# A new order of early loads, and convolution results in two PSUM places in turn

## The reference

```python
xb, wb = sign(layernorm_over_channels(x)), sign(weight)          # 3x3, 64 to 64 channels
conv_sum  = conv(xb, wb)
conv_prod = conv(left * middle * right neighbours of xb, product of wb over its column taps)  # 3x1
x = x + 0.5 * (conv_sum - conv_prod)
t = tokens(x)                                                     # 16 x 1024 tokens of 64
u = layernorm(t)
route: mean of u over the image @ Wr + br -> softmax -> capacity relief -> softmax -> top 2 of 8
y = sum over the 2 experts of weight * (gelu(u @ W1[e] + b1[e]) @ W2[e] + b2[e])
out = t + layernorm(y + u) * gamma + beta
```

## Time and profile before

| | us |
|---|---|
| median of 3 runs | 156.91 (155.15 to 156.95) |
| the profiled execution | 156.77 |
| its span, from the first instruction to the last | 155.0 |
| TensorE busy | 138.1 (89%) |
| ScalarE, VectorE, GpSimd busy | 98.4, 97.3, 47.0 |
| mean TensorE clock that was granted | 0.985 of full speed |

### The profile page before, as it was taken

How to read it: one execution, slowest core, us unless ns; L and a number is a source line. 1 busy time by engine, 2 the same in 40 slices (tenths; PEclk the granted TensorE clock), 3 DMA queues, 4 the chain that set the end, 5 groups by cost and what they waited for, 6 DMA issues and landing times.

```text
span 155.0 us, 2614 instructions
## 1 busy us (share of the span) xinstructions
PE 138.1 (89%) x749; PEld 46.9 (30%) x749; DVE 97.3 (63%) x248; ACT 98.4 (64%) x171; POOL 47.0 (30%) x61
## 2 busy tenths in 40 slices
PE   6794957996998989976799999999999999999990
PEld 2111422331333422323333232333323232333440
DVE  1199232089758787964102288796868777797890
ACT  3398376787545467946666867757575868959321
POOL 8205984966700410001155555645000000000000
PEclk9997799999999999999999999999999999999998
DMA  5998999999975994000025666856691210303007
GB/s 159 346 301 243 247 215 221 209 197 195 174 171 148 367 405 191 0 0 2 25 76 130 155 152 153 191 128 160 156 373 45 93 42 0 135 0 139 1 0 271
DMA packets 14398, 24.09 MB, mean 155 GB/s; under 512 B 3240, under 2 KB 8880, under 8 KB 14384
## 3 DMA queue, kind: packets, MB, share of 16 engines
q1 hardware_dynamic: 13088, 19.67, 45.5%
q0 software_dynamic: 1152, 4.19, 11.2%
q10 hardware_dynamic: 144, 0.07, 0.2%
HBM read 10.80 MB, written 4.19 MB: 97 GB/s over the span
## 4 chain that ended last, share of the span: by engine, by line
PE 63%; DVE 13%; DMA 8%; ACT 5%; issue 3%; POOL 2%; SPq 2%; ACTq 1%; DVEq 0%
PE ps L603 19%; PE ps L615 19%; PE ps L442 7%; PE ps L471 6%; DMA stack<-signs 5%; DMA xs<-in_crossed 4%; DVE us L1010 3%; PE ps L631 3%; DVE us L1005 2%; PE ps L420 2%; ACT signs L709 2%; POOL signs L297 2%; PE ps L647 2%; PE ps L642 2%; DVE stat L978 1%
## 5 line engine op out<-in xcount | busy, mean ns | idle before, releaser
L831 ACT ACTIVATE signs<-ps,b1sel 128x512 f32<-128x512 f32 x64 | 39.5, 687 | 21.1 <-PE ps L603 21.1
L603 PE MATMUL ps<-us,w1sel 64*128 64x512 f32 x128 | 31.8, 615 | 1.4 <-ACT w1sel L819 1.4
L615 PE MATMUL ps<-signs,w2sel 128*64 128x512 f32 x128 | 31.0, 605 | 0.0
L442 PE MATMUL ps<-stack,cwT 128*64 128x512 fp8e4 x192 | 24.9, 406 | 5.6 <-DMA stack<-signs 2.7
L1005 DVE TENSOR_TENSOR us<-us,ps 128x512 f32<-128x512 f32 x16 | 10.5, 679 | 16.4 <-PE ps L452 16.4
L731 ACT ACTIVATE sq<-us 128x1024 f32<-128x1024 f32 (+1 forms) x18 | 17.2, 960 | 4.0 <-DVE us L1005 3.8
L297 POOL TENSOR_TENSOR signs<-edge,signs 128x1024 fp8e4<-128x1024 f16 x7 | 14.5, 2073 | 9.0 <-DVE edge L292 8.7
L1118 DVE SCALAR_TENSOR_TENSOR us<-ps,b2sel,us 128x1024 f32<-128x1024 f32 (+1 forms) x9 | 10.5, 1165 | 9.9 <-PE ps L615 9.9
L442 PEld LDWEIGHTS ps<-stack,cwT 128*64 128x64 f16 x192 | 11.1, 115 | 18.4 <-DMA stack<-signs 7.7
L892 POOL TENSOR_TENSOR w2sel<-w2f,picks 128x64 f32<-128x64 f32 x32 | 11.8, 387 | 15.7 <-issue 11.9
L719 ACT ACTIVATE conv<-ps 128x512 f16<-128x512 f32 x16 | 9.5, 593 | 9.8 <-PE ps L442 9.8
(11 more groups left out here) (109 smaller groups left out, 132.6 us busy)
## 6 DMA issues: line engine op xcount, KB each, us to landing
xs<-in_x SPq DMA_DIRECT2D x8, 512.0 KB, 7.6
xs<-conv POOLq DMA_DIRECT2D x8, 512.0 KB, 4.2
xs<-in_crossed SPq DMA_DIRECT2D x7, 512.0 KB, 6.3
out<-xs SPq DMA_DIRECT2D x6, 512.0 KB, 3.3
stack<-signs SPq DMA_DIRECT2D x16, 144.4 KB, 6.3
stack<-signs SPq DMA_DIRECT2D x14, 144.5 KB, 5.6
out<-xs SPq DMA_DIRECT2D x4, 256.0 KB, 2.2
w1sel<-in_L_ffn_W SPq DMA_DIRECT2D x28, 32.0 KB, 2.4
```

Of the source, the lines that this page charges most:

```text
L442: mm = nc.tensor.matmul(conv_ps[p][IMG[b], h, :], cwT[:, b, r, t, :], rows[:, at:at + ROWS_HALF, t:t + W], start=(r == 0 and t == 0), stop ...
L603: mm = nc.tensor.matmul(hid_ps[b][:, h, :], w1sel[IMG[b], k, p, :], us[IMG[b], p, h * HALF:(h + 1) * HALF], start=True, stop=True)
L615: mm = nc.tensor.matmul(y_ps[IMG[b], h, :], w2sel[:, k, b, p, :], hid[:, k, b, h * HALF:(h + 1) * HALF], start=(k == 0), stop=(k == 1), sk ...
L831: nc.scalar.activation(hid[:, k, b, h * HALF:(h + 1) * HALF], hid_ps[b][:, h, :], ACT.Gelu, bias=b1sel[:, col:col + 1]).then_inc(s_gelu, 1)
```

## The change

There are four parts.

1. **Loads.** Only pairs 1 and 2 are loaded at the start. The load of pair p + 2 moves into stack_pair(p), for p from 1 on, between the transfers of the signs and those of the image's own part. The signs' transfers no longer wait for the product; the own part comes last and does. As load_weights(4) is issued ahead of stack_pair(5), the load of pair 7 is now behind it.
2. **Conv weights.** ScalarE takes two of the steps of `cwT`, behind signs_of(1); VectorE does the rest of them ahead of edges(1).
3. **PSUM.** `CONV_BANK` gives the results of pairs 0 to 7 their first bank: 2, 5, 2, 5, 2, 0, 2, 0. convolve(p) waits for residual(p - 2), or for what else used its banks. spread(0) and spread(3) lie in banks that results now use, so they wait for residual(3) and residual(5).
4. **Order.** On TensorE centre(3) moves behind convolve(0), and the first half of convolve(p + 1) ahead of centre_conv(p); the end of the first part is put in another order. signs_of on ScalarE follows, and edges(3) on VectorE moves behind residual(0).

```diff
+CONV_BANK = (2, 5, 2, 5, 2, 0, 2, 0)
...
-        conv_ps = [ps[:, b:b + 2, :] for b in (2,) * (PAIRS - 1) + (0,)]
+        conv_ps = [ps[:, b:b + 2, :] for b in CONV_BANK]
...
             sp.wait_ge(s_x0[0], 16)
-            for p in range(2, 4):
-                sp.dma_start(xs[:, p, :], crossed[p]).then_inc(s_x[p], 16)
+            sp.dma_start(xs[:, 2, :], crossed[2]).then_inc(s_x[2], 16)
...
-                sp.wait_ge(s_prod, p)
+                sp.wait_ge(s_sign, p)
                 if p >= 3:
                     sp.wait_ge(s_conv, 2 * (p - 2))
                 for b in range(2):
+                    stack_signs(p, b)
+                if p + 2 < PAIRS:
+                    load_x(p + 2)
+                sp.wait_ge(s_prod, p)
+                for b in range(2):
                     stack_own(p, b, (0, 1))
-                    stack_signs(p, b)
 
             for p in range(PAIRS):
                 stack_pair(p)
-                for q in ((4, 5), (6,), (7,))[p] if p < 3 else ():
-                    load_x(q)
                 load_weights(p)
...
                 if p == 0:
-                    pe.wait_ge(s_cw_done, 5)
+                    pe.wait_ge(s_cw_done, 3)
+                    pe.wait_ge(s_cw_act, 2)
                 for h in halves:
-                    if 1 <= p < PAIRS - 1:
-                        pe.wait_ge(s_xc, 2 * (p - 1) + h + 1)
+                    if p == 1:
+                        pe.wait_ge(s_keep, 2)
+                    elif p == 5:
+                        pe.wait_ge(s_keep, PAIRS)
                     elif p == PAIRS - 1:
                         pe.wait_ge(s_dev, 1)
+                    elif p >= 2:
+                        pe.wait_ge(s_xc, 2 * (p - 2) + h + 1)
...
                 if p == 0:
-                    pe.wait_ge(s_keep, 2)
+                    pe.wait_ge(s_xc, 8)
                 elif p == 3:
-                    pe.wait_ge(s_keep, PAIRS)
+                    pe.wait_ge(s_xc, 12)
...
-            for p in range(4):
+            for p in range(3):
                 for h in range(2):
                     centre(p, h)
+            convolve(0)
             for p in range(4):
-                convolve(p)
-
-                centre(p + 4, 0)
-                centre(p + 4, 1)
+                centre(p + 3, 0)
+                centre(p + 3, 1)
+                convolve(p + 1, (0,))
                 centre_conv(p, 0)
                 centre_conv(p, 1)
                 if p == 2:
                     variances(0)
                 elif p == 3:
                     spread(0)
-
-            convolve(4, (0,))
+                convolve(p + 1, (1,))
+
+            centre(7, 0)
+            centre(7, 1)
             spread(1)
-            convolve(4, (1,))
             centre_conv(4, 0)
+            centre_conv(4, 1)
             variances(1)
-            centre_conv(4, 1)
             convolve(5)
+            convolve(6, (0,))
             centre_conv(5, 0)
             centre_conv(5, 1)
-            convolve(6, (0,))
+            spread(2)
+            convolve(6, (1,))
+            spread(3)
             variances(2)
-            spread(2)
-            spread(3)
-            convolve(6, (1,))
             centre_conv(6, 0)
-
-            convolve(7, (0,))
             centre_conv(6, 1)
-            convolve(7, (1,))
+
+            convolve(7)
             centre_conv(7, 0)
             centre_conv(7, 1)
             spread(4)
...
+                elif p == 1:
+                    for b in range(2):
+                        act.wait_ge(s_cw_sign, 1)
+                        nc.scalar.activation(cwT[IMG[b], 1 - b, :, 1, :], cws[IMG[b], 2, :, :], ACT.Copy,
+                                             scale=0.5).then_inc(s_cw_act, 1)
             keep_conv(0)
-            signs_of(4)
+            signs_of(3)
             square(0)
             keep_conv(1)
-
-            signs_of(5)
+            signs_of(4)
             keep_conv(2, (0,))
             square(1)
             keep_conv(2, (1,))
-            signs_of(6)
+            signs_of(5)
             root(0)
             square(2)
             keep_conv(3)
-            signs_of(7)
+            signs_of(6)
             square(3)
             keep_conv(4)
+            signs_of(7)
             square(4)
             root(1)
             keep_conv(5)
...
             conv_weights_early()
+            conv_weights_late()
             edges(1)
-            conv_weights_late()
-            for p in range(2, DVE_EDGES + 1):
-                edges(p)
+            edges(2)
             for p in range(4):
                 residual(p)
+                if p == 0:
+                    edges(3)
                 if p == 2:
                     inverse_deviations(0)
             tokens(0)
```

More of the change, by code:

```diff
@@ L227, in metaformer @@
         s_cw_prep = sem("conv_weight_steps")
+        s_cw_act = sem("conv_weights_scaled_by_act")
         s_cw_done = sem("conv_weights_ready")
@@ L938, in conv_weights_late @@
                                                    in1=cws[IMG[b], 2, :, :], op0=ALU.mult, op1=ALU.mult).then_inc(s_cw_done, 1)
-                    nc.vector.tensor_scalar(cwT[IMG[b], 1 - b, :, 1, :], cws[IMG[b], 2, :, :], 0.5, None,
-                                            ALU.mult).then_inc(s_cw_done, 1)
             steps = [0]
```

## The result

| | before | after |
|---|---|---|
| median | 156.93 us (155.15 to 158.42) | 164.81 us (163.13 to 169.24) |
| profiled execution | 156.77 us, span 155.0 | 163.13 us, span 161.3 |
| mean granted clock | 0.985 | 0.955 |

The ratio is 1.046 (95% interval 1.029 to 1.063): the change makes the kernel slower, by 7.9 us in the medians and 6.4 us between the two profiles.

A forecast was written before the change was run, and what follows sets the result against it. TensorE was taken as the bound, busy 138.1 of 155.0 us, with only the first part's end movable. Adding 1.2 at spread(0), 0.9 in the middle and 4.0 at the end to 156.77 gave 162.9 us, range 159.6 to 166.8.

The forecast's parts named there:

- Part 5: From centre_conv(5) to the last centre_conv(7): two covers removed, TensorE idle 3.4 and 2.6 us; 13.5 us instead of 9.5.
- part 4: From spread(0) to centre_conv(5, 1): 9.3 us of work plus waits of 0.8 for load 7 and 0.4 at convolve(5).
- part 3: Up to spread(0): inverse_deviations(0) takes 5.4 us, then residual(3) 1.25; spread(0) starts at 39.1 against 37.94.
- part 2: The loads: stack 1 lands at 19.6, a lead of 2.3 us; stacks 2 and 3 follow at 25.0 and 30.4.
- the other way of part 2: Stack 3 reckoned through residual(0), edges(3), its product, two issues and landing: 29.8 or later.
- The beat of 5.4 us: Time from one stack to the next, kept from the kernel before because the DMA share was already full.
- its own signs: Profile checks: convolve(0) near 14, variances(0) not before 31.6; wrong if stacks 2 and 3 land near 23 and 28.
- part 1: The start: weights ready near 12, but stack 0 lands at 13.6 to 14.2; no gain taken, bound 0.5 us.
- Rival (a): The two new waits at the end both lower TensorE's clock: 2 x 1.45 us more, 165.8; chance 0.22.
- (b): The new load order gives no lead, as stack pieces behind a load land late: +2.3 us, 165.2; chance 0.08.
- (c): The 2.3 us lead lasts and only the end costs 4.0: 158.5, no measurable change; chance 0.15.
- (d): Two PSUM places close two thirds of TensorE's 5.0 us of gaps from 18 to 57 us: 153.4; chance 0.05.

The follow-up runs named there:

- e2: The kernel after, with 13 empty matmuls ahead of spread(2) and 9 ahead of centre_conv(6, 1): 161.05 us, ratio 1.033.
- e3: The kernel after, with refine(1) moved ahead of residual(5) on VectorE and nothing else: 159.57 us, no ratio.
- e1: The kernel after, with TensorE's old order restored from convolve(5) on: 155.47 us, ratio 0.995; the same kernel in a later job, 157.89 us.
- e4: The kernel before, with only the two PSUM places and the waits that go with them: 157.94 us, ratio 1.013.
- e5: The kernel of e1 with SP's old program too (old load order, each stack wholly behind its product): 159.01 us, ratio 1.033.
- e10: The kernel of e5 with edges(3) back ahead of residual(0) on VectorE: 158.62 us beside 156.79, no ratio.
- e8: The kernel of e1 with 2, 4 and 8 empty matmuls behind the centring of pairs 0, 1 and 2: 155.88 us beside 156.39, no ratio.

## Why the prediction was right, and where it was not

**Right: the direction and its cause.** Part 5 said that the new order at the end uncovers two chains, with waits of 3.4 and 2.6 us; they measured 3.25 and 2.27. Its sum for the stretch, 13.5 us, is near the 13.2 that e2 shows with the clock kept up. e3 takes the first cause away and e1 both; the second alone is read from rows. The two added waits of part 4 measured 0.41 and 0.38 (0.8 and 0.4 forecast), and part 3's inverse_deviations 5.43 us (30.69 to 36.12; 5.4 forecast) and 1.25 for residual(3).

**Wrong by a term: part 2.** I had stack 1 landed at 19.6 and then kept 5.4 us from stack to stack because the transfers' share was full. convolve(1) started at 18.68 without a wait, 1 us ahead of the forecast. convolve(2) started at 24.23, held by load 4 in front of centre(4) and not by its stack, and convolve(3) at 28.70, 4.5 us later, where the forecast had 25.0 and 30.4. What stack 3 waited for is seen in SP's rows, first its signs and then, after 3.1 us of waiting for product 3, its own part:

```profile
20.02 1.27 SPq L342 DMA_DIRECT2D stack<-signs  x2
...
25.04 1.11 SPq L347 DMA_DIRECT2D stack<-signs  x2
```

So it was the other way of part 2 that held: residual(0) was over at 21.8, product 3 at 25.0, the issues at 26.2, each 1 us earlier than forecast because convolve(1) was. In e1 the landing, 2.5 us after the issues, released convolve(3) at 28.19. The beat of 5.4 us had met the same forecast by chance. variances(0) began at 30.69, not 32.45, and centre_conv(5) ended at 47.7, not 49.6. By its own signs the prediction was wrong here: it asked for convolve(0) near 14 and variances(0) not before 31.6, and called itself wrong if stacks 2 and 3 landed near 23 and 28; stack 3 had landed at 28.2 in e1, and stack 2 by 24.2.

The share from 18 to 57 us fell from 0.99 to 0.85. The page of the kernel before, and then that of the kernel after, have for the stack transfers of 144 KB, with the median time to landing last:

```profile
stack<-signs SPq DMA_DIRECT2D x16, 144.4 KB, 6.3
stack<-signs SPq DMA_DIRECT2D x14, 144.5 KB, 5.6
```

```profile
stack<-signs SPq DMA_DIRECT2D x16, 144.4 KB, 3.2
stack<-signs SPq DMA_DIRECT2D x14, 144.5 KB, 3.1
```

A full share did not mean that the next stack had to take as long. Why the landing was faster stays open: with the old program of SP e4 has 4.1 and 3.4, e5 3.1 and 2.7 and e10 3.4 and 2.8 in these two rows, so the order on SP is not shown to be the cause.

**Wrong by a term: part 1.** "I take no gain": convolve(0) started at 13.0, not near 14, and at 12.84 and 12.59 in the two profiles of e1; my bound of 0.5 was too small. The forecast that the wait would go to the stack transfer was right: with the weights early and the old loads it was stack 0 that released convolve(0), at 13.34 in e5 and 14.18 in e10. What I left out is that load 3 no longer stands ahead of stack 0. The pieces of stack 0 of 72 KB landed in a median of 2.3 us in the kernel after (2.3 and 2.1 in the two of e1), and in 3.0, 3.1, 3.3 and 4.0 in the kernel before, e4, e5 and e10; only e8, with the new loads, has 3.3 too. A part is scatter: in e4, which has the program of the kernel before up to there, convolve(0) started at 13.36 and not at 14.24. Of the 1.2 us, 0.4 went again into convolve(0), 4.74 us at the low clock.

**The clock.** Rival (a), with a chance of 0.22, came true: 2.9 us forecast, 2.9 measured. My reason against it, dense work around both waits, did not hold. That the two sizes agree is in part chance: the two convolutions lost 1.25 and 1.15 us, not 1.45 each, and small operations beside them the rest. So the forecast of 162.9, beside 163.13 in the profile, is near by luck too: it was 1.9 us too late before the end and 2.6 too short in it, and behind the mark it took 97.4 us and not 98.0. The median, 164.81, is further off.

**Rivals (b), (c), (d).** (b) fell: there was a lead. (c) came about in half: a true lead of 1.2 to 1.4 us lasted until the end. But its sum, 158.5, sets a lead against 4.0 us and leaves out the 1.4 of the half convolution that the main sum has in its middle; by the prediction's own prices it is 159.9. With the clock the end cost 8.1. (d) fell by e4, and e5 and e10 agree.

## What to carry to other kernels

Before an order is changed, list for each product that is waited for what stands between its last input and its use, and price the cover that goes; here 0.5 us of waits for the single place was removed, and the order that gave up the cover cost 8 us. When a start comes earlier, count the work that was postponed: 3.9 us of lead was 1.4. And a wait in TensorE costs twice when the clock falls behind it. Behind waits of 2 to 3 us it fell in some profiles and not in others, so such a wait is to be priced both ways.

## What the runs showed of the hardware

- TensorE's granted clock fell to 0.50, the 1.2 GHz level, behind waits of 2.27 and 3.25 us (kernel after), 2.25 (e3), 2.30 (before, ahead of convolve(0)) and 3.53 (e4). It stayed at full speed behind 1.76 (before), 1.92 (e5), 2.18 (e4) and, ahead of convolve(0) in e4, 2.76. Empty matmuls in the waits of e2 kept it up, which was worth 2.9 us.
- The median landing time of the same 144 KB stack transfers was between 2.7 and 6.3 us under one and the same program of SP (e5 and the kernel before), and 3.2 and 3.1 in the kernel after.
- An operation of VectorE with 32 elements in each partition, L971, took 1.40 and 1.66 us in the kernel after, each time until a product of GpSimd was over (33.97 and 33.95, 46.03 and 45.99), and 0.18 when GpSimd was idle. The first of them and the product beside it:

```profile
32.57 1.40 DVE L971 TENSOR_SCALAR stat<-var_t 128x32 f32<-128x32 f32 x1
```

```profile
32.00 1.95 POOL L299 TENSOR_TENSOR signs<-edge,signs 128x1024 fp8e4<-128x1024 f16 x1
```

The Trainium skill (SBUF — State Buffer, Who interferes with whom) calls the port pair that the two share an exclusive lock, held for a whole instruction; these rows agree. Not every operation of VectorE is held: two of L1016 took 1.28 us at 26.11, beside GpSimd's edges (25.55 to 27.44), and 1.28 at 20.57 with GpSimd idle.
